# Three PSUM banks for the score products and three for the ring of the other stages, with new step lists

## The reference

```python
xn = _layernorm(x, axis=-1)
s = _L0_attn_ref(xn, ...)      # 16 heads of 16
g = _silu(_L0_ffn_ref(xn, ...))
...
# in _L0_attn_ref
scores = jnp.take(causal_kern, jnp.maximum(doff, 0), axis=-1)
scores = scores + qm[..., :, None] + km[..., None, :]
scores = scores + MIX * jnp.einsum('bhic,bhjc->bhij', qc, kc) / math.sqrt(CR)
scores = jnp.where(causal, scores, -1000000000.0)
attn = jax.nn.softmax(scores, axis=-1)
ctx = jnp.einsum('bhij,bhjd->bhid', attn, v)
...
h = _ln(x + attn_out, ln1_g, ln1_b)
ffn = jax.nn.gelu(h @ ffn_w1 + ffn_b1, approximate=False) @ ffn_w2 + ffn_b2
return _ln(h + ffn, ln2_g, ln2_b)
...
# in _L0_ffn_ref: fp4_linear quantises both operands in blocks of 16
gate = fp4_linear(x, w_gate)
y = fp4_linear(x, w_up)
h = jax.nn.silu(gate) * y
return fp4_linear(h, w_down)
```

## Time and profile before

| | |
|---|---|
| three executions | 1926.29, 1918.35 and 1924.22 us, median 1924.22 |
| span of the profiled execution | 1916.1 us |
| outside that span, against the median | 8.1 us |
| instructions | 37547 |
| DMA | 166.69 MB, mean 87 GB/s |

### The profile page before, as it was taken

The page is one execution under the profiler, slowest core; times in us unless marked ns, Lnnn a source line. Parts: engine busy times, 40 slices in busy tenths (PEclk is TensorE's granted clock), DMA queues, the critical chain, the costliest instruction groups (busy, mean ns, idle before and its releaser), DMA issues.

```text
span 1916.1 us, 37547 instructions
## 1 busy us (share of the span) xinstructions
PE 1822.3 (95%) x12803; PEld 1311.7 (68%) x12803; DVE 1590.4 (83%) x5143; ACT 930.2 (49%) x1939; POOL 1095.4 (57%) x797
## 2 busy tenths in 40 slices
PE   7888999999999999999999999999999999999987
PEld 3335677777767767676776767677776767677766
...
GB/s 156 165 96 114 64 91 83 75 110 75 99 75 79 76 82 115 75 90 73 91 74 93 93 75 110 64 102 79 83 77 75 110 84 91 75 85 74 61 57 34
DMA packets 138646, 166.69 MB, mean 87 GB/s; under 512 B 19757, under 2 KB 100654, under 8 KB 138452
## 3 DMA queue, kind: packets, MB, share of 16 engines
...
...
## 4 chain that ended last, share of the span: by engine, by line
PE 50%; DVE 26%; issue 12%; POOL 4%; DMA 3%; ACT 3%; SPq 2%; DVEq 0%; POOLq 0%; ACTq 0%
PE ps L760 8%; PE ps L769 7%; PE ps L701 7%; PE ps L718 4%; DVE Pr L1067 3%; PE ps L624 3%; PE ps L597 3%; PE ps L733 3%; PE ps L658 3%; PE ps L674 2%; DVE nmax L1037 2%; POOL slot L1215 2%; PE ps L654 2%; DMA Tz<-kernel_rows 2%; DVE st L958 2%
## 5 line engine op out<-in xcount | busy, mean ns | idle before, releaser
L1176 POOL TENSOR_TENSOR Pr<-Pr,Tz 128x768 f32<-128x768 f32 (+2 forms) x384 | 477.6, 1273 | 233.8 <-ACT Pr L833 230.0
L1037 DVE CUSTOM_DVE_ANT_0 ps<-ps,future 128x512 f32<-128x512 f32 (+3 forms) x1024 | 474.5, 516 | 52.9 <-issue 51.8
L833 ACT ACTIVATE Pr<-ps 128x384 f32<-128x384 f32 x512 | 243.1, 489 | 345.2 <-PE ps L658 343.9
L760 PE MATMUL ps<-catT,w 128*128 128x256 f32 x1024 | 237.8, 380 | 0.7 <-ACT catT L896 0.7
L769 PE MATMUL ps<-w,gT 128*128 128x256 f32 x1024 | 232.9, 381 | 0.9 <-ACT gT L913 0.9
L624 PE MATMUL ps<-KS,QS 108*128 108x512 bf16 (+3 forms) x1024 | 215.0, 300 | 17.9 <-DVE nmax L1037 13.2
L822 ACT ACTIVATE ps<-ps 128x512 f32<-128x512 f32 x256 | 150.5, 588 | 137.7 <-PE ps L654 136.1
L1067 DVE SCALAR_TENSOR_TENSOR Pr<-ps,Tz 128x512 f32<-128x512 f32 x256 | 175.3, 685 | 46.2 <-ACT ps L822 41.0
L769 PEld LDWEIGHTS ps<-w,gT 128*128 128x128 f32 x1024 | 190.8, 190 | 25.7 <-ACT gT L913 1.3
L760 PEld LDWEIGHTS ps<-catT,w 128*128 128x128 f32 x1024 | 189.6, 190 | 26.2 <-ACT catT L896 0.9
L718 PE MATMUL ps<-wdT,hqT 128*128 128x256 f32 x768 | 179.5, 383 | 0.7 <-ACT hqT L872 0.7
...
## 6 DMA issues: line engine op xcount, KB each, us to landing
Tz<-kernel_rows SPq DMA_DIRECT2D x256, 256.0 KB, 3.6
...
```

What stands on the lines that cost most here:

```text
L760: ins = mm(dst[:, i * n:(i + 1) * n], w1[:, c, f * P:(f + 1) * P], catT[:, c, hf * n:(hf + 1) * n], start=c == 0, stop=c == KD - 1)
L833: inc(af(Pr[:, p % 4, e, at:at + wd], src[:, 0:wd], ACT.Exp), "a_exp")
L1037: ins = v.tensor_tensor_reduce(o, o, future[:, S - n:S], -1.0, 3e38, ALU.add, ALU.min, nmax[:, 2 * pl + e, it:it + 1])
L1176: ins = g.tensor_tensor(a, a, Tz[:, p % 2, :, P * j:P * j + PAST[j]], ALU.mult)
```

## The change

The first ring gets bank 2 from the third: the score products have banks 0, 1 and 2, the other stages 3, 4 and 5. Unit n of the scores now waits for unit n-3, which makes bank 0 the bank of all diagonal units. In the third ring a use waits for the use three before it. As 56 is no multiple of 3, a step has another bank in each pass; `psum_plan` now runs through all the batches one by one, and the functions look the bank up by batch.

```diff
+TURNS = [("head", 0)] + [("mid", b) for b in range(1, B - 1)] + [("end", B - 1)]
...
 def psum_plan(orders, kinds, banks):
-    uses = {p: [(w, u) for w, s in orders[p] for u in kinds(s)] for p in PARTS}
...
-        assert tail["head"].get(b, (0, 0))[1] == tail["mid"][b][1], "banks differ between iterations"
...
+    uses = [(at, u) for p, at in TURNS for w, s in orders[p] for u in kinds(s) for at in [at if p == "mid" else PARTS[p][w]]]
+    ahead = sum(len(kinds(s)) for w, s in orders["head"])
+    place, before, last = {}, {}, {}
+    for i, (at, u) in enumerate(uses):
+        bank = banks[(i - ahead) % len(banks)]
+        place[at, u] = bank
+        if bank in last:
+            before[at, u] = last[bank]
+        last[bank] = (u, at)
     return place, before
...
-        SC_BANKS, B_BANKS, C_BANKS = [0, 1], [6, 7], [2, 3, 4, 5]
+        SC_BANKS, B_BANKS, C_BANKS = [0, 1, 2], [6, 7], [3, 4, 5]
...
-        def bank_for(ring, released, eng, u, which, b):
+        def bank_for(ring, released, eng, u, b):
             place, before = plans[ring]
-            if (which, u) in before:
-                earlier, ago = before[which, u]
-                released(eng, earlier, b + ago)
-            return ps[:, place[which, u], :]
+            if (b, u) in before:
+                released(eng, *before[b, u])
+            return ps[:, place[b, u], :]
```

All the lists of `ORDER` are laid out anew, on every engine and in the head, the middle and the end. They hold the same steps as before. Of the middle list of TensorE, its first line:

```diff
-            cT out.0 out.1 sc.0.0 gu.0.0 sc.0.1 gu.0.1 sc.0.2 sc.0.3 mx.1.0.0 mx.1.0.1 sc.0.4 gu.1.0 sc.0.5 mx.1.0.2
+            cT out.0 out.1 sc.0.0 sc.0.1 sc.0.2 gu.0.0 gu.0.1 mx.1.0.0 sc.0.3 sc.0.4 sc.0.5 mx.1.0.1 sc.1.0 sc.1.1
```

More of the change, by code:

```diff
@@ L84 @@
[L84 to L88, removed]
+            pre:iota pre:half pre:rs.0 pre:rs.1 pre:rs.2 pre:rs.3 pre:ones pre:rs.4 pre:rs.5 pro:projm.0 pre:wm.0.0
@@ L101 @@
[L101 to L105, removed]
@@ L171 @@
+            hr.2 mul.6 fin hq.3 mul.7 hr.3
         """,
         vector="""
-            out.0 out.1 ln1 muld.0.0 silu.0.0 lnc1 silu.0.1 muld.0.1 mx.1.0.0 lnb1 mx.1.0.1 mx.1.0.2 muld.1.0 mx.1.0.3
-            silu.1.0 mx.1.0.4 mx.1.1.0 muld.1.1 mx.1.1.1 mx.1.1.2 mx.1.1.3 mx.1.1.4 muld.2.0 mx.1.2.0 mx.1.2.1 hq.0
-            mx.1.2.2 mx.1.2.3 norm mx.1.2.4 mx.1.3.0 muld.2.1 mx.1.3.1 mx.1.3.2 mx.1.3.3 mx.1.3.4 muld.3.0 mfin.1 hr.0
-            silu.1.1 f2.0 muld.3.1 proj.0 hq.1 f2.1 ctxt.0 proj.1 proj.2 muld.4.0 hr.1 xq muld.4.1 xr xr2 silu.2.0
@@ L177 @@
-            muld.5.0 silu.2.1 hq.2 v.0 v.1 muld.5.1 f2.2 hr.2 mx.0.0.0 mx.0.0.1 f2.3 ln2 mx.0.0.2 mx.0.0.3 muld.6.0
-            silu.3.0 ctxt.1 muld.6.1 lnc2 lnb2 mx.0.0.4 mx.0.1.0 dn.0 silu.3.1 muld.7.0 mx.0.1.1 mx.0.1.2 mx.0.1.3
-            mx.0.1.4 hq.3 muld.7.1 mx.0.2.0 mx.0.2.1 mx.0.2.2 mx.0.2.3 mx.0.2.4 dn.1 ctxt.2 hr.3 mx.0.3.0 mx.0.3.1
-            dn.2 mx.0.3.2 mx.0.3.3 mx.0.3.4 mfin.0 ctxt.3 dn.3
+            out.0 out.1 ln1 lnc1 silu.0.0 muld.0.0 lnb1 muld.0.1 mx.1.0.0 silu.0.1 mx.1.0.1 mx.1.0.2 muld.1.0 mx.1.0.3
@@ L224 @@
-            last:ctxt.2 last:ctxt.3 tail:out.0 tail:ln1.0 tail:out.1 tail:lnc1.0 tail:lnb1.0 tail:ln1.1 tail:lnc1.1
-            last:dn.3 tail:lnb1.1 tail:f2.0 tail:f2.1 tail:ln2.0 tail:lnc2.0 tail:lnb2.0 tail:f2.2 tail:f2.3
-            tail:ln2.1 tail:lnc2.1 tail:lnb2.1
+            last:silu.0.0 last:out.0 last:muld.0.0 last:out.1 last:ln1 last:lnc1 last:silu.0.1 last:muld.0.1
+            last:mx.1.0.0 last:lnb1 last:silu.1.0 last:muld.1.0 last:mx.1.0.1 last:mx.1.0.2 last:hq.0 last:muld.1.1
@@ L227 @@
+            last:silu.3.1 last:muld.6.0 last:hq.3 last:f2.3 last:muld.6.1 last:dn.1 last:muld.7.0 last:hr.3
+            last:muld.7.1 last:ctxt.1 last:ln2 last:lnc2 last:dn.2 last:lnb2 last:ctxt.2 last:ctxt.3 tail:out.0
+            tail:ln1.0 tail:lnc1.0 tail:lnb1.0 tail:out.1 tail:ln1.1 last:dn.3 tail:lnc1.1 tail:lnb1.1 tail:f2.0
+            tail:f2.1 tail:ln2.0 tail:lnc2.0 tail:f2.2 tail:lnb2.0 tail:f2.3 tail:ln2.1 tail:lnc2.1 tail:lnb2.1
         """,
         tensor="""
[L229 removed]
```

289 lines of the change are left out of this document (141 added, 148 removed).

## The result

The changed kernel takes 2110.74 us (median of four executions, 2109.2 to 2111.93) against 1922.62 us of the kernel before in the same session (four, 1918.35 to 1926.29). The ratio is 1.0979, interval 1.0956 to 1.1002: slower by 188 us, far outside the range that was forecast. A pass of the middle list takes 122.9 us where it took 109.8, and 14 times 13.1 us is 183 us: nearly all of the loss lies in the repeated list. The head is 8.8 us longer too: TensorE starts its first `hT` at 256.5 us where it was 247.7.

A forecast was written before the change was run, and what follows sets the result against it. TensorE was taken as the bound, busy 1822.3 of 1916.1 us, VectorE a close second. Terms -26.8 - 7.5 + 26.6 + 7 = -0.7 us gave 1923 us, no change; 8-in-10 range 1896 to 1946.

The forecast's parts named there:

- The score waits go: TensorE's 45 waits of score products for `muld` and exponentials all vanish, with lost overlap counted: 26.8 us saved.
- a new wait at the start of a pass: `sc.1.0` waits for bank 0 until VectorE ends `muld.0.1`: 1.9 us a pass, 26.6 us over 14.
- `hT`, 7.5 us: TensorE's `hT` stops waiting for the layer norm, as `lnb1` comes earlier on VectorE: 15 x 0.5 = 7.5 us saved.
- `mT`, 7 us for `mT.1` and nothing for `mT.0`: `mT.1` newly waits for the later `mfin.1`, 0.5 us in 14 passes; `mT.0` at the pass end adds nothing.
- Two more table loads, nothing: ScalarE gets two more 1.28 us table loads per pass, with no cost to the time.
- the cover: At `gu.2.0`, ScalarE frees the bank after 9.1 us and TensorE needs it after 9.65: 0.5 us of slack.
- nothing in its new order is asked for by TensorE early: GpSimd's reordered list was taken as harmless, with 45 us free per pass; no cost given.
- `lnc1` 1.66 less 0.08 of overlap, 1.58: `lnc1`'s time in the VectorE row before `muld.0.1` at the start of a pass; the row sums to 7.48 us.
- The third ring causes no wait that shows: In the trace before, `gu` follows `gu` and scores without a gap, so that ring showed no TensorE wait.
- Head and end: The first 232 us and last 146 us: same steps reordered, taken as 0, with 5 us to either side.
- Rival (b): Slower: VectorE becomes the bound of a pass, 1.5 us per pass, 21 us in all, 1945 us; chance 0.21.

The follow-up runs named there:

- run 10: run 9 plus GpSimd's `xr` ahead of `hq.2` and `mul.5` behind `ln2`, and VectorE's `lnc2` behind `mx.0.1.0`; 2003.9 us.
- run 3: The changed kernel with one GpSimd step, `xnb`, moved behind `mul.0` in the middle list; 2063.6 us.
- run 7: run 6 plus ScalarE's `sc.4.3` and `sc.4.4` moved behind `f1.1.3`, one table change per pass in place of three; 2033.2 us.
- run 6: run 3 plus GpSimd's `xr` ahead of `mul.5`, `hr.2` ahead of `ln2` and `mul.6` behind `fin`; 2037.1 us.
- run 2: The changed kernel's banks and head with the middle and end lists of the kernel before, except three `silu` steps moved earlier; 2264.1 us, ratio 1.1765.
- run 5: The kernel before with one GpSimd step, `xnb`, moved ahead of `mul.0` in each middle pass; 2010.3 us, ratio 1.0458.
- run 9: run 7 with VectorE's `mx.0.0.2` moved ahead of its `hr.2`; 2031.4 us.

## Why the prediction was wrong

The steps of the prediction, one by one.

- *"The score waits go", 26.8 us.* Half right. Line 646 waits for nothing any more. But with the new lists line 642 waits 25.0 us, against 19.6 for both kinds in the earlier trace rows, and still 21.0 in run 10. The bank moved the wait and did not remove it. About half of that was forecast as "a new wait at the start of a pass", 1.9 us. With `xnb` out of the way (run 3) `gu.0.1` waits 0.80 us and `sc.1.0` 0.90; with the 0.16 of overlap that the prediction adds to each, 2.0 together. There place, mechanism and size were right.
- *`hT`, 7.5 us:* right for the passes, and too large: the trace of before has 12 such waits, 4.1 us in all (line 750), 6 with their overlap. One new wait of 3.2 us stands in the last batch, to which the sum gave nothing.
- *`mT`, 7 us for `mT.1` and nothing for `mT.0`.* Line 620 waits 15.1 us, 29 times: `mT.1` 0.62 us a pass and `mT.0` 0.44. The cast of `mfin` is one of the lengthened instructions, 0.78 us as a median (line 1038) where it was 0.27.
- *Two more table loads, nothing.* ScalarE's 36 us are there; run 7 against run 6 gains 4 us net without two of them per pass. That the cover held is not refuted, and not shown: in run 7 another wait came in.
- **The step that failed** is the sentence on GpSimd: "nothing in its new order is asked for by TensorE early". True and beside the point. It looked at who waits for GpSimd, and not at who works beside it. Every VectorE term of the sum, above all "`lnc1` 1.66 less 0.08 of overlap, 1.58", took a duration from the old neighbourhood into a new one. `lnc1` became 3.79 us and `lnc2` 6.43; 1.9 us of wait at the start of a pass became 2.88 and more, and every long pause was paid a second time in clock, of which the sum had no term at all.
- *A second step that failed:* "The third ring causes no wait that shows", from which its lost bank was priced at one place, 0.7 us inside a wait that swallows it. With the old lists that bank is worth far more (159.6 us of waits in run 2), and with the new ones and most of the stretching gone `gu` still waits at three places of a pass (run 10: 0.80, 1.13 and 1.09 us).
- *Head and end, 0 with 5 us to either side:* the head alone is 8.8 us longer, which the prediction named as a sign of being wrong. No run takes it apart.
- *Rival (b)*, VectorE the bound with TensorE waiting for maxima, names the right engine, and its own sign came (passes above 110.5 us with such waits). It was priced at 1.5 us per pass; it was 13.1, since it counted pauses of VectorE and not longer instructions or the clock.

The Trainium skill has the rule that the sum lacked ("SBUF — State Buffer", SBUF: two separate sides): VectorE's second port pair is GpSimd's only one, is held for a whole instruction, and the other engine stands still meanwhile; it names VectorE operations with two SBUF inputs or in a two-port mode. The traces agree in the main: what was left of `xnb` is waited for, 1.89 us in run 5; `muld`, with one input in PSUM, is never longer than 693 ns; and the plain `TENSOR_SCALAR` of `hr.2` is stretched, 0.53 to 2.03 us (whether it runs in such a mode no trace shows). One row does not fit it: the second product of `lnc1` lies wholly beside GpSimd's `rstd` of 1.02 us, in every pass, and takes 0.47 us.

What makes up the 188 us: taking four stretched places apart (runs 3, 6 and 10) gives 47.2 + 26.5 + 27.5 us, with 3.9 for the tables and 1.8 from run 9, in all 107; the last two are too small to be told from nothing. Of the 81 that are left at 2003.9 us, 14 x (115.1 - 109.8) = 74 lie in the passes. The third ring's 44 waits at line 689 (28.3 + 15.3 = 43.6 us; none before), 13.8 more at line 620 (1.3 before) and 11.4 more for maxima come to 68.8. So waits for a bank of the third ring are the largest piece of the remainder. Two of their three places came with the edits (`gu.2.1` with run 7, the wait for line 1115 with run 10), and the waits of line 620 are in another ring. This is read from the waits and not shown by a run: no two kernels that were run with the new lists differ in that bank alone. VectorE's busy time is also still 53.6 us over that of before, and may hold some of these waits. No version tried beats the kernel before.
